# Layer 0, first batch: the query projection between the key ones, the raw query weights in a room of their own, values that don't wait for queries, and all stack copies issued by SyncE

## The reference, cut to what matters

```
h = concatenate([ctx, x])                     # 512 key rows of 512 features
q = (x @ q_w + q_b)                           # 256 query rows
k, v = (h @ kv_w + kv_b)                      # 512 rows each, interleaved columns
attn = softmax(mask(q k^T / 32))              # 16 heads, 256 x 512 each
y = attn v @ out_w + out_b + x
y = rmsnorm(y); out = gelu(y @ w1 + b1) @ w2 + b2 + x
```

## Time and profile before

| | us |
|---|---|
| median of 3 runs | 2380.22 |
| lowest and highest run | 2379.0, 2381.1 |
| the profiled execution, its own time | 2378.66 |
| its span, first to last instruction | 2376.9 |
| TensorE busy in it | 2332.7 (98%) |
| ScalarE, VectorE busy | 1478.9 (62%), 1161.8 (49%) |
| mean granted TensorE clock | 0.992 |

### The profile page before, as it was taken

How to read it: one execution, slowest core, us unless ns; L and a number is a source line. 1 busy time by engine, 2 the same in 40 slices (tenths; PEclk the granted TensorE clock), 3 DMA queues, 4 the chain that set the end, 5 groups by cost and what they waited for, 6 DMA issues and landing times. The chain is left out here.

```text
span 2376.9 us, 43895 instructions
## 1 busy us (share of the span) xinstructions
PE 2332.7 (98%) x14670; PEld 1899.4 (80%) x14670; DVE 1161.8 (49%) x2246; ACT 1478.9 (62%) x3458; POOL 297.3 (13%) x336
## 2 busy tenths in 40 slices
PE   7999999999999999999999999999989999999998
PEld 6777777777777777678888888888878888888886
DVE  5555555556665655633122122122156666666674
ACT  4877777877777787753222222222248778787886
POOL 1111011111111011310000000000131221212110
PEclk9999999999999999999999999999999999999998
DMA  7344444444444444632010010011144545545443
GB/s 209 91 117 110 110 106 106 107 108 106 106 106 113 116 116 98 156 108 74 33 53 30 23 53 36 17 53 44 45 137 135 148 133 146 136 141 148 135 125 89
DMA packets 148193, 239.11 MB, mean 101 GB/s; under 512 B 25600, under 2 KB 59680, under 8 KB 148144
## 3 DMA queue, kind: packets, MB, share of 16 engines
q1 hardware_dynamic: 146224, 235.31, 36.4%
q10 hardware_dynamic: 1920, 3.15, 0.6%
HBM read 86.28 MB, written 25.21 MB: 47 GB/s over the span
## 5 line engine op out<-in xcount | busy, mean ns | idle before, releaser
L750 ACT ACTIVATE score_ps<-score_ps,l_neg_max 128x512 f32<-128x512 f32 (+1 forms) x1024 | 567.4, 560 | 117.9 <-DVE l_neg_max L1001 116.2
L1001 DVE TENSOR_REDUCE l_neg_max<-score_ps 128x1 f32<-128x512 f32 (+1 forms) x768 | 494.9, 684 | 48.2 <-PE score_ps L1278 46.5
L1725 ACT ACTIVATE mlp_hidden<-score_ps,b_col 128x512 f32<-128x512 f32 x128 | 88.3, 690 | 503.8 <-PE score_ps L67 458.2
L1773 DVE TENSOR_TENSOR mlp_hidden_l<-mlp_hidden,mlp_hidden_h 128x512 fp32r<-128x512 f32 x128 | 92.7, 724 | 518.6 <-ACT mlp_hidden_h L1727 518.5
L65 PE MATMUL item_ps<-feats_h,weights_l 128*128 128x256 f32 (+1 forms) x1024 | 323.3, 316 | 6.3 <-DVE weights_l L924 4.5
L770 ACT ACTIVATE l_probs<-score_ps 128x1024 f32<-128x1024 f32 x272 | 270.6, 1020 | 78.0 <-PE score_ps L1313 76.0
L66 PE MATMUL item_ps<-feats_l,weights_h 128*128 128x256 f32 (+1 forms) x1024 | 319.0, 311 | 0.0
L67 PE MATMUL item_ps<-feats_h,weights_h 128*128 128x256 f32 (+1 forms) x1024 | 318.2, 311 | 0.0
L1278 PE MATMUL score_ps<-l_stack 97*128 97x512 f32 (+1 forms) x1024 | 300.6, 361 | 13.5 <-ACT score_ps L750 10.0
L1313 PEld LDWEIGHTS score_ps<-l_stack 99*128 99x128 f32 x1536 | 213.1, 192 | 47.6 <-issue 16.9
L1313 PE MATMUL score_ps<-l_stack 99*128 99x256 f32 x1536 | 245.2, 292 | 3.6 <-ACT score_ps L750 1.4
(11 more groups left out here) (161 smaller groups left out, 4126.9 us busy)
## 6 DMA issues: line engine op xcount, KB each, us to landing
l_stack<-room SPq DMA_DIRECT2D x248, 192.0 KB
l_stack<-l_qk SPq DMA_DIRECT2D x252, 128.0 KB
l_stack<-l_qk SPq DMA_DIRECT2D x252, 64.0 KB
l_stack<-room SPq DMA_DIRECT2D x124, 128.0 KB
l_tokens<-in_x SPq DMA_DIRECT2D x16, 512.0 KB, 3.4
l_tokens<-in_ctx SPq DMA_DIRECT2D x16, 512.0 KB, 4.2
l_rows<-in_x SPq DMA_DIRECT2D x16, 512.0 KB, 4.1
norm_transposed<-norm_room SPq DMA_DIRECT2D x16, 512.0 KB, 4.8
```

Source lines behind the costliest of these rows:

```text
L750: m = act.activation(e, e, ACT.Exp, bias=neg_max[:, q, h:h + 1], accum_out=row_sum[:, q, h:h + 1])
L1001: dve.tensor_reduce(out, bank, AXIS_X, ALU.max, negate=True).then_inc(max_done, 1)
L1725: act.activation(hidden[:, m % HBUF, :], hidden_ps[:, m % 4, :], ACT.Gelu_apprx_tanh, bias=b1_col[:, m:m + 1])
L1773: dve.tensor_tensor(hidden_p[1][:, m % HBUF, :], hidden[:, m % HBUF, :], f32(hidden_p[0][:, m % HBUF, :]), ALU.subtract).then_inc(hidden_l ...
```

## The change

In layer 0 the items get a table, `KIND`: token items 0 to 3, then key 0, key 1, query 0, key 2, key 3, query 1. That holds for the first batch and for all others. The q weights are loaded right behind kv into `probs_room[:, 2:4]`, with a semaphore of their own, and split second; the o weights take the place of the first half of kv once split 4 is done, behind the store of the mask rows. The first half of the stack needs the lows of key 0, key 1 and query 0 (7 lows, before 9), the second all 10 (as before). All its DMAs for batch 0 are SyncE's. `v_share` of batch 0 doesn't wait for the lows. The score steps of iteration 1 start in slot 1: `[0, 2, 4, 2, 2, 2, 2, 6, 6, 6]`. The instructions of layer 1 and of the perceptron are as they were.

```diff
--- before.py
+++ after.py
@@ -253,6 +253,10 @@
+    KIND = ([("tokens", f) for f in range(NT)]
+            + ([("key", 0), ("key", 1), ("query", 0), ("key", 2), ("key", 3), ("query", 1)] if first
+               else [("both", g) for g in range(NK)]))
@@ -260,7 +264,7 @@
-    STEPS_AT_FIRST = [0, 0, 0, 2, 2, 2, 2, 8, 8, 8] if first else [2, 2, 2, 2, 2, 2, 2, 2]
+    STEPS_AT_FIRST = [0, 2, 4, 2, 2, 2, 2, 6, 6, 6] if first else [2, 2, 2, 2, 2, 2, 2, 2]
@@ -368,8 +373,12 @@
-        stage = ([probs_room[:, 0:2, :].rearrange("p a b -> p (a b)"), v[:, :, :].rearrange("p a b -> p (a b)")] if first
-                 else [room[:, 0, :], room[:, 2, :]])
+        stage = ([probs_room[:, 0:2, :].rearrange("p a b -> p (a b)"), v[:, :, :].rearrange("p a b -> p (a b)"),
+                  probs_room[:, 0:2, :].rearrange("p a b -> p (a b)"),
+                  probs_room[:, 2:4, :].rearrange("p a b -> p (a b)")] if first
+                 else [room[:, 2 * (u % 2), :] for u in range(4)])
+        raw_sem = [raw_loaded[0], raw_loaded[1], raw_loaded[0], q_loaded if first else raw_loaded[1]]
+        raw_count = [16, 16, 32, 16 if first else 32]
@@ -379,15 +388,16 @@
             split_ops = []
-            for which, w in ((0, wk), (1, wv)):
...
+            for which, w in ((0, wk), (None, wq), (1, wv), (None, wo)):
...
@@ -400,19 +410,18 @@
-            SPLITS_OF_K, SPLITS_OF_V, SPLITS_OF_Q = 2, 4, 6
+            SPLITS_OF_K, SPLITS_OF_Q, SPLITS_OF_V = 2, 4, 6
             FIRST = (T_ITEMS + [("split", n) for n in range(4)] + K_ITEMS[:2] + [("split", 4)] + K_ITEMS[2:3]
-                     + [("split", 5)] + K_ITEMS[3:] + [("split", 6), ("split", 7)] + Q_ITEMS)
+                     + [("split", 5)] + K_ITEMS[3:4] + [("split", 6)] + K_ITEMS[4:5] + [("split", 7)] + K_ITEMS[5:])
@@ -481,11 +490,11 @@
-        FIRST_OF_ACT = [(HG - 2, HG - 1), (HG - 2, HG - 1) if first else ()]
+        FIRST_OF_ACT = [() if first else (HG - 2, HG - 1), ()]
 
         def lows_of(p, half):
 
-            return ITEMS * p + (NT + NK + half + 1 if first else NT + GROUPS * (half + 1))
+            return ITEMS * p + NT + (3 if first else GROUPS) * (half + 1)
@@ -493,24 +502,24 @@
             def load_raw(u):
-                sp.dma_start(raw_view(u), raw[u]).then_inc(raw_loaded[u % 2], 16)
+                sp.dma_start(raw_view(u), raw[u]).then_inc(raw_sem[u], 16)
 
             if first:
 
                 load_tokens(sp, 0)
                 load_raw(0)
                 load_raw(1)
+                load_raw(3)
             with nc.allow_non_contiguous_dma(reason="per-feature vectors, once"):
                 for dst, src in vectors_to_load():
                     sp.dma_start(dst, src).then_inc(vec_loaded, 16)
             if first:
                 sp.dma_start(mask_raw, mask_src).then_inc(mask_loaded, 16)
-                for u in (3, 2):
-
-                    sp.wait_ge(w_low, last_op_of[u - 2] + 1)
-                    load_raw(u)
                 sp.wait_ge(mask_made, 1)
                 sp.dma_start(mask_rows, mask_tile).then_inc(mask_stored, 16)
+
+                sp.wait_ge(w_low, last_op_of[0] + 1)
+                load_raw(2)
@@ -890,11 +899,6 @@
-                    if first and n == ITEMS - 1:
-                        for half in range(HALVES):
-                            act.wait_ge(low_done, NT + NK + half + 1)
-                            for j in FIRST_OF_ACT[half]:
-                                move_stack(act, stack_of(0), half, j, range(SPLIT))
@@ -1249,8 +1253,6 @@
                 at_first = isinstance(b, int) and b == 0
                 if f == 0:
-                    if at_first:
-                        pe.wait_ge(low_done, ITEMS)
                     at_least(pe, o_norm_done, FB * b)
@@ -1479,7 +1481,7 @@
                         pe.wait_ge(w_low, SPLITS_OF_K)
-                    if n == NT + NK:
+                    if n == KIND.index(("query", 0) if first else ("both", 0)):
                         pe.wait_ge(w_low, SPLITS_OF_Q)
```

More of the change, by code:

```diff
@@ L381, in attention_layer @@
             split_ops = []
-            for which, w in ((0, wk), (1, wv)):
-                for c in range(2):
-                    kv = stage[c].rearrange("p (f n two) -> p f n two", f=2, two=2)
-                    split_ops.append((c, kv[:, :, :, which], [t[:, 2 * c:2 * c + 2, :] for t in w], 1.0))
-            for u, w, scale in ((3, wq, SCALE), (2, wo, 1.0)):
-                src = stage[u % 2].rearrange("p (f n) -> p f n", f=FB)
+            for which, w in ((0, wk), (None, wq), (1, wv), (None, wo)):
                 for c in range(2):
                     part = slice(2 * c, 2 * c + 2)
-                    split_ops.append((u, src[:, part, :], [t[:, part, :] for t in w], scale))
+                    if which is not None:
+                        kv = stage[c].rearrange("p (f n two) -> p f n two", f=2, two=2)
+                        split_ops.append((c, kv[:, :, :, which], [t[:, part, :] for t in w], 1.0))
+                    else:
+                        u, scale = (3, SCALE) if w is wq else (2, 1.0)
+                        src = stage[u].rearrange("p (f n) -> p f n", f=FB)
+                        split_ops.append((u, src[:, part, :], [t[:, part, :] for t in w], scale))
         else:
@@ L705, in split_high @@
                 if first:
[L706 removed]
+                    act.wait_ge(raw_sem[u], raw_count[u])
                 else:
@@ L727, in high @@
                     n = act.activation(hT[0][:, k, :], ps[:, :], ACT.Copy)
-                elif not first:
-                    g = k - NT
+                elif KIND[k][0] == "both":
+                    g = KIND[k][1]
                     at_least(act, stack_loaded[g // GROUPS], 16 * STACK_DMAS * b)
@@ L1201, in item @@
                 else:
-                    g = k - NT
-                    if not first:
+                    kind, g = KIND[k]
+                    if kind == "both":
                         parts = [(wq, g), (wk, g)]
-                    elif g < NK:
+                    elif kind == "key":
                         parts = [(wk, g)]
                     else:
-                        parts = [(wq, 2 * (g - NK)), (wq, 2 * (g - NK) + 1)]
+                        parts = [(wq, 2 * g), (wq, 2 * g + 1)]
                     width = 2 * S // len(parts)
```

28 lines of the change are left out of this document (14 added, 14 removed).

## The result

The changed kernel takes 2384.72 us (median of 10 runs, 2383.47 to 2387.98), the kernel before 2380.32 in the same comparison (10 runs, 2374.63 to 2383.47). The ratio is 1.0028, 95% interval 1.0020 to 1.0035: slower by 6.7 us (4.8 to 8.3), where 2.1 were forecast. The plain difference of the two medians is only 4.4 us, just outside this interval; against the median of the 109 further runs of the kernel before that were taken with the experiments (2378.3) it is 6.4. I go by the ratio. The profiled execution took 2387.74 us, one of the longest of the ten, so its absolute end is no measure of the median. What I compare are moments of the first 83 us, and above all the start of the second pass.

What follows compares the result with a forecast made beforehand. TensorE, 98% busy, was taken to bound the kernel, with only the first 75 us movable. Item 0 of batch 1 6.1 us later, less 4.0 for six fewer steps, gave +2.1: 2380.2 + 2.1 = 2382.3 us, range 2375.5 to 2386.0.

Steps and rivals of the forecast that it cites:

- First stack copy at 27.9: SyncE's queue: the first stack copy is issued at 27.9 us, where it was 33.20.
- 10.7 us, to 43.0, and 0.6 us for landing and release, my allowance: 43.6: Stack's first half, behind o and tokens until 32.3: 2.36 MB at 221 GB/s, so the first score can start at 43.6.
- Idle time 6.9 us: TensorE ahead of its first score: waits for the stack from 36.7 to 43.6, 6.9 us.
- the same slow stretch: TensorE behind the stack wait: half clock for 3.5 us as before, 1.75 us lost.
- 24 value matmuls and six scores, 6.87 us with the clock up: TensorE from first score to item 0 of batch 1: 5.47 us of values plus 1.4 of scores, clock loss apart.
- Six steps fewer later, 4.0 back: Slots 7 to 9 of the first pass: six score steps fewer, each worth 0.67 us, give 4.0 us back.
- The wait of 1.93 us: TensorE ahead of the value share: this wait for the last query's lows, and 1.75 us lost behind it, are gone.
- The loop neutral: Later batches: a query's high part takes 0.84 us instead of 0.69, item 8 gives 0.15 back; costed at nothing.
- Rival 4: Loop not neutral: the query's 0.15 us comes through in 14 batches, 2.1 us more, +4.2 in all; chance 0.09.
- Rival 3: Early loads: the q load delays kv's second half, all moves by up to 2.6 us, +4.7; chance 0.10.
- Rival 1: Stack's first half early, at 40.9, limited by its issuing: -0.6 us, or -2.4 if the clock stays up; chance 0.18.
- Rival 2: Behind the first score engines pack better, only TensorE's work counts: -2.9 us, -5.6 with rival 1's stack; chance 0.14.

Runs made afterwards that it cites:

- f4: The changed kernel, but SyncE issues the stack's second half only after the first half has landed; ratio 1.0024 to the kernel before.
- f1: The kernel before, with only the value share of batch 0 no longer waiting for the lows; ratio 1.0018 to the kernel before.
- h3: The changed kernel with 48 useless matmuls ahead of value row 0 and item 3's transposes in batch 1 done four times; ratio 1.0012 to the kernel before.
- g2: The changed kernel with o loaded early into free rooms and batch 1's tokens early, so nothing stands ahead of the stack; ratio 1.0006 to the kernel before.
- f2: The changed kernel with batch 1's tokens loaded behind the stack's first half and the old score steps put back; ratio 1.0015 to the kernel before.
- f5: f1 with 16 useless matmuls behind item 0 of batch 1, in the gap ahead of the first score; ratio 0.9985 to the kernel before.
- h1: The kernel before with 9 useless matmuls ahead of the value share, while it waits for the lows; ratio 0.9994 to the kernel before.

## Why the prediction was wrong

The sign was right, and so was the path: the change makes the kernel slower because the first score, with all behind it, waits for the stack. The size of the wait was not. The forecast was +2.1 us; measured were +6.7. Its steps in order:

- **First stack copy at 27.9:** 27.43. Right.
- **"10.7 us, to 43.0, and 0.6 us for landing and release, my allowance: 43.6":** this is the step that failed. The score started at 47.16, 3.6 us later. The bytes were nearly right: the slices from 24 to 43 us sum to 4.34 MB, and o, tokens and half 0 have 4.46. What was missing is the uneven end: the allowance of 0.6 for landing and release is what f4 shows behind its last byte (46.25 to 46.82), but that byte is the last engine's. In the changed kernel the last increment comes at 47.02, 1.5 us behind all but two of them. In f4 the same arithmetic gives 28.36 + 15.7 = 44.1 against 46.8; of these 2.8 us some 1.5 are the uneven end (my estimate above), the other 1.3 stay open. The rest of the miss in the change, up to 1.3, can be the copies behind. The Trainium skill ("DMA: Bandwidth & Descriptors", the section on queues, rings and completion order) says that the increment of a semaphore lands only after every earlier write of that DMA engine; by this each engine has to work off its own share of the 2.1 MB and of the copies first, and f4's uneven end agrees. My rows held a better estimate: from first issue to first score before, 13.3 us (with two issuers, and f1 shows that the half landed just then), plus the loads ahead in full, 2.1 MB at 406 GB/s = 5.2, gives 27.9 + 18.5 = 46.4. I had reached that value only as the far end ("a stack at 46.3 and later") and given it 0.03.
- **Idle time 6.9 us:** 11.2. The value share also ended 0.7 us earlier than the 36.7 forecast: it starts at 33.07, not at 34.0.
- **"After it I take the same slow stretch: 1.75 us lost (...) an idle time three times as long has no reason to cost less":** it cost more. Item 0 came 9.33 us behind the first score, 7.01 with the clock up (h3): 2.3 lost. A second stretch, which I didn't foresee, cost 1.2 in the profile (26.07 against 24.88 from item 0 to second pass). The clock terms together: 1.75 forecast, 3.5 in the profile.
- **24 value matmuls and six scores, 6.87 us with the clock up:** 7.01 in h3. Right. **Six steps fewer later, 4.0 back; 24.6 us from item 0 to the second pass:** 24.9 in h3. Right.
- **The wait of 1.93 us "and the slow stretch behind it are gone":** right as a fact. f1 shows that there was nothing to gain in it: alone, it costs 4.3 us.
- **The loop neutral:** 0.08 us a batch shorter, 1.1 in all; which instruction gives it, no run shows. Rival 4 had the other sign.
- **Second half by 54, o and the vectors in time, key 0 not disturbed:** right, the half but for its last 0.05 MB, which end by 56; key 0 starts at 14.76 (14.64 before) and no wait for the second half shows. Rival 3 is false. Rival 1 is false even with an empty queue (g2: 14.35 us from issue to score, not 13.0). Rival 2, better packing, is seen nowhere.

The sum with the measured terms: 2.1 + 3.6 (stack) + 0.7 + 1.5 (item 0 and the second pass later than forecast by the clock, in the profile) - 1.1 (loop) = 6.8, against 6.7. That it fits to 0.1 is luck: the interval is 3.5 us wide, and for f2 and f5 the same kind of sum misses.

## What to carry to other kernels

Before a dependent chain is moved up behind a DMA, price the landing by the whole time from first issue to first use in a trace, and add in full whatever stands ahead of it in the queue; bytes over bandwidth ends too early by the uneven finish of the engines. Ahead of a transfer that comes late anyway, removing a wait gains nothing, and can lose where the idle time, and with it the slow clock, moves up against the critical chain: taking the slow stretch away from plain work, as h1 did, brought the second pass no earlier, so idle time is best left there. Here the fix was to empty the queue, by loading o and the tokens early (o into rooms that were free), and to leave the first score behind the values: g2, with the empty queue alone, is no faster than before.

## What the runs showed of the hardware

- The granted clock went to its lower level behind idle times of 1.93 us (before) and 3.5 us (f1), just after the first matmul, and stayed there for some 3.3 us; an idle time of 1.74 us (h1) left it up. In the idle time of 11.2 us (the change) it fell at 38.5, 2.5 us in, and did not come back with the first matmul: it stayed at 0.50 for another 5 us of work.
- Copies of the stack within the core's memory ran at 200 to 250 GB/s with all engines full, loads at up to 410 GB/s in the same queue. A queue that mixes them shows both rates side by side in the slices (315, 229, 240, 400, 306).
- A half of the stack behind 2.1 MB of loads ended with one engine alone for 1.1 us (f4); behind none, the last twelve increments came within 0.3 us (g2).
- One program's executions differ by 5 us and more, and their mean granted clock goes with it (0.996 and 2375.2 us, 0.992 and 2379.8): the two traces of which windows are shown have slow stretches of different length where a layer ends. Differences of 1 to 4 us between kernels need moments within the trace beside the medians.
